# Turning the gathered token rows of a mixture-of-experts kernel by a transposing DMA instead of TensorE

## What is computed

```python
x = x + jnp.tanh(g_xattn[0]) * _L0_xattn_ref(ctx, ctx, _layernorm(x, axis=-1), ssm_kernel, D, 8)
x = x + jnp.tanh(g_ffn[0]) * _L0_ffn_ref(_layernorm(x, axis=-1), gate_w, w1, w2, w3, sw1, sw2, sw3)

# _L0_ffn_ref, 2048 tokens t of 512, 16 experts of 352, top 2, and a shared expert of 704
scores = jax.nn.softmax(t @ gate_w.T, axis=-1)
weights, indices = jax.lax.top_k(scores, TOP_K)
for e in range(N_EXPERTS):
    w_e = jnp.sum(jnp.where(indices == e, weights, 0.0), axis=-1)
    y = y + _swiglu(t, w1[e], w3[e], w2[e]) * w_e[:, None]     # (silu(t @ wa.T) * (t @ wb.T)) @ wo.T
z = _swiglu(t, sw1, sw3, sw2)
return (y + z).reshape(shape)
```

## Time and profile before

| | us |
|---|---|
| median of 3 runs | 742.87 |
| lowest, highest | 742.52, 745.36 |
| span of the profiled execution | 739.8 |
| PE busy | 717.1 (97%) |
| DVE busy | 568.5 (77%) |
| ACT busy | 459.4 (62%) |
| POOL busy | 363.4 (49%) |
| DMA, queue of SP | 89.67 MB, 37.1% of 16 engines |
| DMA, queue of POOL | 24.40 MB, 17.9% of 16 engines |

### The profile page before, as it was taken

One profiled execution on the slowest core, in us unless ns is written; L12 is line 12 of the kernel. 1 busy time (PEld: TensorE's weight loads), 2 busy tenths in 40 slices (PEclk: granted clock), 3 DMA queues, 4 the chain that ended last, 5 costly groups with the idle time before them and its releaser, 6 DMA issues.

```text
span 739.8 us, 15553 instructions
## 1 busy us (share of the span) xinstructions
PE 717.1 (97%) x4602; PEld 676.3 (91%) x4602; DVE 568.5 (77%) x1111; ACT 459.4 (62%) x659; POOL 363.4 (49%) x190
## 2 busy tenths in 40 slices
PE   3999999999999999999999999999999999999998
PEld 3999999999998999899989999988989999999997
DVE  7899999999965578428899588848987699679942
ACT  6575757575432222126878588847885789578931
POOL 4999888887401065042435433543634354434320
PEclk9999999999999999999999999999999999999999
DMA  6678687877522122463667577766565764432101
GB/s 231 215 239 288 218 272 216 279 218 253 186 85 60 29 43 29 144 197 90 161 201 218 131 232 210 198 176 168 145 182 160 176 193 90 74 68 46 30 1 57
DMA packets 48404, 114.88 MB, mean 155 GB/s; under 512 B 7472, under 2 KB 8624, under 8 KB 48336
## 3 DMA queue, kind: packets, MB, share of 16 engines
q1 hardware_dynamic: 35792, 89.67, 37.1%
q0 software_dynamic: 12544, 24.40, 17.9%
HBM read 157.78 MB, written 29.26 MB: 253 GB/s over the span
## 4 chain that ended last, share of the span: by engine, by line
PE 69%; DVE 13%; DMA 6%; issue 5%; ACT 3%; SPq 1%; ACTq 1%; POOL 1%; DVEq 1%; POOLq 0%
PE pair L1303 19%; PE bank L1303 15%; PE pair L1328 12%; PE pair L1234 8%; PE bank L1328 6%; PE bank L1185 4%; PE pair L1311 3%; DMA out<-ys,slot_info 3%; DMA raw<-in_weights 2%; PE bank L1245 2%; DVE prod L829 2%; DVE bank L834 2%; DVE x L800 2%; DVE w_lo L1150 1%; DVE rows L841 1%
## 5 line engine op out<-in xcount | busy, mean ns | idle before, releaser
L1150 DVE TENSOR_TENSOR w_lo<-raw,w_hi 128x1408 fp32r<-128x1408 f32 x94 | 148.5, 1621 | 47.0 <-ACT w_hi L733 47.0
L1441 POOL DMA_INDIRECT out<-ys,slot_info x47 | 80.6, 1714 | 120.6 <-ACT ys L721 87.3
L1428 POOL DMA_INDIRECT tn<-t_rows,slot_info x47 | 75.5, 1605 | 123.1 <-DVE tT_lo L888 90.6
L733 ACT ACTIVATE w_hi<-raw 128x1408 fp32r x94 | 124.6, 1374 | 2.1 <-issue 1.4
L1234 PE MATMUL pair<-kv_hi,toep_hi 128*128 128x288 f32 x320 | 100.6, 314 | 1.7 <-DMA toep_lo<-kpad_lo 1.4
L1234 PE MATMUL pair<-kv_lo,toep_hi 128*128 128x288 f32 x320 | 95.3, 298 | 0.0
L1234 PE MATMUL pair<-kv_hi,toep_lo 128*128 128x288 f32 x320 | 95.1, 297 | 0.0
L1155 DVE TENSOR_TENSOR w_lo<-raw,w_hi 128x1536 fp32r<-128x1536 f32 x47 | 82.3, 1752 | 4.5 <-ACT w_hi L740 4.5
L1379 POOL TENSOR_TENSOR kv_lo<-kv,kv_hi 128x2304 fp32r<-128x2304 f32 x15 | 77.3, 5153 | 5.9 <-ACT kv_hi L625 5.9
L740 ACT ACTIVATE w_hi<-raw 128x1536 fp32r x47 | 69.3, 1474 | 0.1
L829 DVE TENSOR_TENSOR prod<-pair,q 128x256 f32<-128x256 f32 x128 | 53.4, 417 | 15.1 <-PE pair L1234 9.6
(11 more groups left out here) (223 smaller groups left out, 2009.3 us busy)
## 6 DMA issues: line engine op xcount, KB each, us to landing
raw<-in_weights SPq DMA_DIRECT2D x94, 704.0 KB
raw<-in_weights SPq DMA_DIRECT2D x47, 768.0 KB
toep_hi<-kpad_hi SPq DMA_DIRECT2D x15, 512.0 KB, 4.6
toep_lo<-kpad_lo SPq DMA_DIRECT2D x15, 512.0 KB, 6.2
cx<-in_ctx SPq DMA_DIRECT2D x15, 384.0 KB, 6.3
stage<-in_weights SPq DMA_DIRECT2D x16, 272.0 KB, 6.7
xt<-in_x SPq DMA_DIRECT2D x16, 256.0 KB, 6.4
xr<-in_x SPq DMA_DIRECT2D x16, 256.0 KB, 6.6
```

Source lines behind the costliest of these rows:

```text
L733: act.activation(w_hi[s % 2][:, a:b], raw[:, bass.ds(half + a, b - a)], ACT.Copy).then_inc(hi_ok[n_], 1)
L1150: dve.tensor_tensor(w_lo[s % 2][:, a:b], raw[:, bass.ds(half + a, b - a)], w_hi[s % 2][:, a:b].bitcast(F32), ALU.subtract).then_inc(lo_ok[ ...
L1428: pool.indirect_dma_start(out=tn[o % 3][:], out_offset=None, in_=t_rows, in_offset=bass.IndirectOffsetOnAxis(ap=slot_info[:, 3 * i:3 * i + ...
L1441: pool.indirect_dma_start(out=out, out_offset=bass.IndirectOffsetOnAxis(ap=rows, axis=0), in_=ys[o % 2][:], in_offset=None, bounds_check=R ...
```

## The change

The kernel no longer turns the gathered rows on PE. The steps are now:

1. ACT writes each normalized tile a second time as two planes of half words (`halves_of_words`): the low 16 bits of all 512 numbers, then the high ones. The two copies stand between norm_x and q_copy in the turn of the first stage, the last tile's ahead of the second stage's loop. SP stores these planes, and not t1, to t_rows (2048 rows of 1024 half words).
2. POOL gathers rows of planes into fetched (two buffers), in the step of `last_unit(o - 6)`, and waits for the save that frees the buffer.
3. SP saves fetched to one of four DRAM scratch tensors turn_rows (256 rows of 512 half words: each token gives two rows), in the step of `last_unit(o - 5)`, after the gather has landed.
4. SP issues a transposing DMA from turn_rows into tn, in the step of `last_unit(o - 4)`, after the save has landed. The two half words of each number come to lie side by side, so tn then holds the turned tile.
5. ACT and DVE split the tile from tn, as they do for shared tiles. The four products on PE and the bank that they wrote are gone from this path.

Shared tiles are loaded as before.

```diff
-        t_rows = nc.dram_tensor("t_rows", (ROWS, L), F32, kind="Internal").ap()
+        t_rows = nc.dram_tensor("t_rows", (ROWS, 2 * L), U16, kind="Internal").ap()
+        turn_rows = [nc.dram_tensor(f"turn_rows_{n}", (2 * P, L), U16, kind="Internal").ap() for n in range(TURNS)]
...
+        planes = sb2("planes", [P, 2 * L], U16, one)
+        fetched = [sb(f"fetched{n}", [P, 2 * L], U16) for n in range(2)]
...
+        def begun(o, ahead):
+            return max(last_unit(o - ahead), 15)
...
+        def gathers_at(n):
+            return [o for o in range(len(ORDER)) if ORDER[o][0] and begun(o, 6) == n]
+        def saves_at(n):
+            return [o for o in range(len(ORDER)) if ORDER[o][0] and max(begun(o, 5), 16 if ORDER[o][1] < 2 else 17) == n]
+        def turns_at(n):
+            return [o for o in range(len(ORDER)) if ORDER[o][0] and max(begun(o, 4), 16) == n]
...
+                if which == "t":
+                    wait(sp, planes_ok, (t + 1) * 2)
+                    sp.dma_start(t_t[bass.ds(t.v, 1)].rearrange("x p c -> (x p) c"),
+                                 planes[p][:]).then_inc(t_out[p], 16)
+                    return
...
+                for o in saves_at(n):
+                    i = ORDER[o][1]
+                    sp.wait_ge(row_in[i % 2], 16 * (i // 2 + 1))
+                    sp.dma_start(turn_rows[i % TURNS].rearrange("(p h) c -> p (h c)", h=2),
+                                 fetched[i % 2][:]).then_inc(turn_out[i % TURNS], 16)
+                for o in turns_at(n):
+                    i = ORDER[o][1]
+                    sp.wait_ge(turn_out[i % TURNS], 16 * (i // TURNS + 1))
+                    wait(sp, tTl_ok, o - 2)
+                    sp.dma_start_transpose(tn[o % 3][:].bitcast(U16).rearrange("p (c r) -> p c r", c=BLOCKS),
+                                           turn_rows[i % TURNS]).then_inc(tn_in[o % 3], 16)
...
+            def halves_of_words(t):
+                p = t.odd
+                wait(act, t_out[p], t.half() * 16)
+                wait(act, t_ok, t + 1)
+                for h in range(2):
+                    act.activation(planes[p][:, h * L:(h + 1) * L], view(t1[p][:].bitcast(U16), h, [[2, L]]),
+                                   ACT.Copy).then_inc(planes_ok, 1)
...
-                for o in prepares_at(n):
-                    if ORDER[o][0]:
-                        turn_tile(o)
...
-                wait(pool, tTl_ok, o - 2)
-                pool.indirect_dma_start(out=tn[o % 3][:], out_offset=None, in_=t_rows,
+                if i >= 2:
+                    pool.wait_ge(turn_out[(i - 2) % TURNS], 16 * ((i - 2) // TURNS + 1))
+                pool.indirect_dma_start(out=fetched[i % 2][:], out_offset=None, in_=t_rows,
```

More of the change, by code:

```diff
@@ L27 @@
 U32 = mybir.dt.uint32
+U16 = mybir.dt.uint16
 ALU = mybir.AluOpType
@@ L59 @@
 FINALS = 2
+TURNS = 4
 @dataclass(frozen=True)
@@ L290, in program @@
         r_fields, r_info, r_done = sem("r_fields"), sem("r_info"), sem("r_done")
-        tn_in, row_in = [sem(f"tn_in{n}") for n in range(3)], [sem(f"row_in{n}") for n in range(3)]
+        tn_in, row_in = [sem(f"tn_in{n}") for n in range(3)], sem2("row_in")
+        planes_ok, turn_out = sem("planes_ok"), [sem(f"turn_out{n}") for n in range(TURNS)]
         tn_mid_in = sem("tn_mid_in")
-        tile_turned, tTh_ok, tTl_ok = sem("tile_turned"), sem("tTh_ok"), sem("tTl_ok")
+        tTh_ok, tTl_ok = sem("tTh_ok"), sem("tTl_ok")
         up_ok, silu_ok, hid_ok = sem("up_ok"), sem("silu_ok"), sem("hid_ok")
@@ L322, in unit @@
             return UNITS[n] if 0 <= n < N_UNITS else None
+        def begun(o, ahead):
+            return max(last_unit(o - ahead), 15)
         def fills_at(n):
-            def at(o):
-                return max(last_unit(o - 4), 15 if ORDER[o][0] else 0)
-            return [o for o in range(3, len(ORDER)) if at(o) == n]
+            return [o for o in range(3, len(ORDER)) if not ORDER[o][0] and max(last_unit(o - 4), 0) == n]
+        def gathers_at(n):
[4 more added lines that the diff above has]
+            return [o for o in range(len(ORDER)) if ORDER[o][0] and max(begun(o, 4), 16) == n]
         def prepares_at(n):
@@ L354, in tn_count @@
         def tn_count(o):
-            return 16 * sum(ORDER[k][0] == ORDER[o][0] and k not in MID for k in range(o % 3, o + 1, 3))
+            return 16 * sum(k not in MID for k in range(o % 3, o + 1, 3))
         def last_unit(o):
@@ L460, in store @@
                 p = t.odd
-                to, src, ready, done = {"x2": (out_t, x2, x2_ok, x2_out), "t": (t_t, t1, t_ok, t_out),
-                                        "tT": (tT_t, tT, tT_ok, tT_out)}[which]
+                if which == "t":
[3 more added lines that the diff above has]
+                    return
+                to, src, ready, done = {"x2": (out_t, x2, x2_ok, x2_out), "tT": (tT_t, tT, tT_ok, tT_out)}[which]
                 wait(sp, ready, t + 1)
@@ L596, in norm_x2 @@
                 p = t.odd
-                wait(act, t_out[p], t.half() * 16)
+                wait(act, planes_ok, (t - 1) * 2)
                 wait(act, t_turned, t - 1)
@@ L684, in turn @@
                     norm_x(t + 1)
+                if not first:
+                    halves_of_words(t - 1)
+                if not last:
                     q_copy(t + 1)
@@ L694, in tile_hi @@
                 routed, i = ORDER[o]
-                if routed:
-                    act.wait_ge(tile_turned, i + 1)
-                    src = ps_t
-                elif o in MID:
+                if o in MID:
                     act.wait_ge(tn_mid_in, 16 * (MID.index(o) + 1))
@@ L711, in _ @@
             norm_x2(At(TILES - 1))
+            halves_of_words(At(TILES - 1))
             def weigh_out(o):
@@ L1271, in _ @@
             sum_rows(At(TILES - 1), 3)
-            def turn_tile(o):
-                pe.wait_ge(row_in[o % 3], tn_count(o))
-                wait(pe, tTl_ok, o)
-                turn_rows(tn[o % 3], ps_t, tile_turned)
             def parts(hi, lo, whi, wlo):
@@ L1420, in gather @@
             def gather(o):
-                routed, i = ORDER[o]
-                if not routed:
-                    return
+                i = ORDER[o][1]
                 if i == 0:
                     pool.wait_ge(r_done, 1)
-                wait(pool, tTl_ok, o - 2)
-                pool.indirect_dma_start(out=tn[o % 3][:], out_offset=None, in_=t_rows,
+                if i >= 2:
+                    pool.wait_ge(turn_out[(i - 2) % TURNS], 16 * ((i - 2) // TURNS + 1))
+                pool.indirect_dma_start(out=fetched[i % 2][:], out_offset=None, in_=t_rows,
                                         in_offset=bass.IndirectOffsetOnAxis(ap=slot_info[:, 3 * i:3 * i + 1], axis=0),
-                                        bounds_check=ROWS - 1, oob_is_err=False).then_inc(row_in[o % 3], 16)
+                                        bounds_check=ROWS - 1, oob_is_err=False).then_inc(row_in[i % 2], 16)
             def add_out(o):
@@ L1445, in _ @@
             for n in range(N_UNITS + 3):
-                for o in fills_at(n):
+                for o in gathers_at(n):
                     gather(o)
```

2 lines of the change are left out of this document (1 added, 1 removed).

## The result

The changed kernel takes **795.4 us** (median of 4 runs, 790.5 to 799.5) against 743.0 beside it: a ratio of 1.071, with a 95% interval of 1.067 to 1.076. It is slower by 52 us, where the forecast was 755, 12 slower. The time lies in the range and the sign is right, but the loss is four times the forecast's.

What follows compares the result with a forecast made beforehand. The prediction took PE as the bound, with DVE and weight loads close behind. Gain -16, transfers +7 and added waits +21 sum to +12; with span 739.8 and 3.1 to the median, 755 us, range 727 to 808.

Steps and rivals of the forecast that it cites:

- What bounds before: Routed part: PE's queue sets the end at 6.62 us per unit, with DVE at 6.30 close behind.
- The gain, -16: Routed tiles: dropping PE's 47 x 4 turning products saves 16 us, ends 15 and 20.7.
- What is late next is DVE at 6.30: Routed units: without the turns DVE's 6.30 us round limits each unit's gain to 0.32 us, 15.0 in all.
- The half-word copies, nothing: First stage: ACT's two added copies, 1.2 us per tile, hide in its 2.8 us idle for PE; no cost.
- Two transfers, 0.80 + 1.1: DMA engines, per routed tile: save 0.80 us, transposing load 1.1 (0.80 or 1.42); +7 us from 380 to 484.
- the rival with the dear load: The transposing load holds the DMA engines 3 us or more a tile: 800 us, far end 899; chance 0.15.
- The transposing load itself: nothing of its own: Routed tiles: issued two units, 12.6 us, ahead of ACT's split, so its landing adds no wait.
- The added waits, +21: Gather waits for save, scatter queues behind gather, ACT's ys waits for scatter: +21 us, ends 0 and +49.
- per load: Added waits counted for each of 14 weight loads among routed units: 0 to 3.5 us, taken as 1.5.
- In a quiet unit 3.9 us are left: Away from weight loads, the scatter lands with 3.9 us to spare before ACT wants the ys buffer again.
- what would show it: Signs of being right: gathers waiting for saves, scatter waits above 30.4 us, PE gaps behind weight splits, DMA share above 0.85.
- Mostly from 380 to 550: Sign: new PE gaps ahead of up products, behind weight splits, would lie mostly from 380 to 550 us.

Runs made afterwards that it cites:

- the run without turns: The kernel before without PE's four products per routed tile, nothing else added (routed output wrong): 736.3 us, ratio 0.992.
- the third buffer: The changed kernel with three buffers for fetched rows in place of two, all transfers kept: 769.0 us, ratio 1.032.
- both cures: The changed kernel with three buffers for fetched rows and the save ahead of the step's weight loads: 763.2 us, ratio 1.031.
- three ys: The changed kernel with three buffers ys in place of two, nothing else touched: 778.8 us, ratio 1.048.
- the run with plain loads: The changed kernel with three fetched buffers, the save first, and plain loads of the same bytes for the transposing ones (routed part wrong): 753.6 us, ratio 1.011.
- idle transposing loads: The kernel before without PE's turns, plus a transposing load per routed tile into buffers nobody reads: 748.4 us, ratio 1.008.

## Why the prediction was wrong, step by step

**What bounds before: right as far as it went.** PE was the bound. What stood behind it was ranked wrongly.

**The gain, -16: it was 6.0.** The step that failed is "What is late next is DVE at 6.30". Behind 716 us, where the DMA is quieter, the units of the changed kernel do go at 6.21 to 6.22, the full 0.40 faster, for the seven units that the chain shows there. Elsewhere another thing was late before DVE: the chain of scatters, by the trace of the run without turns. That it ate all that is missing is not shown. The prediction had weighed the row of 30.4 us for the added waits, but not for its first term. That row told how little slack was left, and a gain on the chain spends that slack first.

**The half-word copies, nothing: right.** ACT has 16.1 us more work in the first 209 us (144.3 for 128.2), PE's busy time is the same to 0.3 us, and ACT's wait for PE ahead of the copy to q fell from 45.1 to 30.5 us.

**Two transfers, 0.80 + 1.1: it was 0.80 + 1.9.** The save was sized right, by its mean with a plain load. For the transposing load the bounds of 0.80 and 1.42 were too low; only the far end held it, and 1.9 lies at the point, "about 2 us a tile", from which the rival with the dear load was said to decide. By the prediction's own working, 5.0 + 0.80 + 1.9 = 7.7 for a unit of 6.30 gives 14 x 1.4 = 20 us (17 with 4.8 for 5.0) and not 7. Measured alone, the loads cost 12. The time of 795 is near the 800 of that rival, but it did not come about in the rival's way: tn was waited for once only, and plain loads in the same place still took 778. That the time lies in the range is luck in part, since this rival had set the upper end.

**"The transposing load itself: nothing of its own": half right.** Nobody waited for its tile but once, 7.6 us. But its issue holds SP, where weight loads and saves are queued. Its line in the changed kernel (ns, min/median/max):

```profile
L577 SPq DMA_TRANSPOSE tn<-turn_rows x47: 1237/1412/5536, 323.6 to 741.2; - x47
```

The prediction counted SP's waits at the save and at the load, and no time for the issue. A plain save's issue takes 0.36 us by its median. How much of the 12 us is SP's hold and how much the engines' time was not separated.

**The added waits, +21: right in kind, too small, and the step that failed most.** 26 us by the third buffer, 32 by both cures; without the save 37 come back, which is the waits with the save's own traffic. What failed is the count: "per load", 14 steps with 1.5 us, and "In a quiet unit 3.9 us are left". It took a wait near each weight load and free units between. But POOL waited for a save at 23 of 47 gathers, and ACT for a scatter at 20. A save landed in 2.0 to 10.2 us (2.1 to 4.4 was assumed, from the medians of stores of the first stage, where no scatters run) and a scatter in up to 11.9. So the round is often longer than a unit, as at 403.93 above, and then its rate would count and not a delay that the next idle time swallows; the run that was to tell the two apart, with three ys, fell between them. Nor did the terms add, as the cures overlap and landings came later: over the 51 scatters from the first routed tile on the mean time from issue to landing is 5.36 us before, 5.57 without turns and 6.29 in the changed kernel.

**A term that was missing: the clock.** PE's 4414 products are as many in the changed kernel as in the run without turns, but they keep it busy for longer. The first line of either page, the changed kernel first:

```profile
PE 722.4 (91%) x4414; PEld 676.0 (85%) x4414; DVE 568.2 (72%) x1111; ACT 476.3 (60%) x691; POOL 365.8 (46%) x190
```
```profile
PE 701.4 (95%) x4414; PEld 656.5 (89%) x4414; DVE 567.8 (77%) x1111; ACT 458.4 (62%) x659; POOL 371.4 (51%) x190
```

So of the 59.8 us between the two spans (794.5 and 734.7) 21.0 are slower products and 38.8 are idle time. The mean granted clock is 0.963 and 0.998. The windows below show how. The prediction priced a stall at its own length. This isn't a cause beside the others: the stalls bring it, so it is part of what each cure gave back (with both cures PE is busy 708.3 us).

**What stays open.** With both waits cured the changed kernel is at 758 to 763, 22 to 27 us above 736.3. Some 10 of it are the transposing (the run with plain loads). The rest comes with the save, the loads and the gathers; the runs don't divide it among the engines' time, SP's list and scatters that land later.

Of what would show it: gathers waiting for saves, ACT's waits well above 30.4, PE's gaps behind weight splits and a share above 0.85 all came. The share is a weak sign, since idle transposing loads alone bring 0.90. "Mostly from 380 to 550" did not come: 551 to 698 lost 21 us of PE's work too, against 24 in 351 to 551.

## What to carry to other kernels

When work is taken from the bounding engine, look for the chain that runs just behind it, and price the gain against that chain's period, not against the next engine's busy time. When an operation moves to DMA, ask for each of its transfers whose list it stands in, what is queued behind it there, and whether the round that it closes (buffer, landing, next issue) takes longer than one unit; if it does, multiply by all units. A further buffer at the tightest place of such a round is a cheap test; here it gave back more than any other single edit that kept the transfers.

## What the runs showed of the hardware

A transposing load of 256 KB of half words took 1.87 us of sixteen engines' time, in 1056 packets of 248 bytes on average, where a save or a plain load of as many bytes took 0.80 in 144 packets, by the mean of the two. In the changed kernel its issue held SP's queue 1.2 us at least and up to 5.5. Where nobody waited for it, it landed 3.2 to 15.2 us after issue (5.5 by the median). The Trainium skill, Advanced Engine Details and Errata, X-Bar Transpose (TRN2), calls such a load as fast as a regular one: here it took 2.3 times the engine time. The Trainium skill, VectorE: DVE Perf Modes, The three transpose paths, gives 1309 ns for a block by DMA; the eight blocks of a tile are an estimate of 10.5 us by that page. Here that lies among the slow landings and far above the 1.87 us of engine time.

A gap on PE cost more than its length. Here is one in the changed kernel. ACT comes to ys 6.15 us late, for a scatter; its hi parts and DVE's lo parts of the weights are late by that, and PE idles 5.29 us for them. Timeline of ACT and of PE, and windows of 3 us (columns as in the earlier trace rows, the granted clock is the third number from the end):

```profile
585.74 0.69 ACT L765 ACTIVATE ys<-bank,slot_info 128x512 f32<-128x512 f32 x1 [6.15 <-DMA out<-ys,slot_info]
591.38 0.93 PE L1342 MATMUL bank<-w_hi,tT_hi 128*128 128x352 f32 x2 [5.29 <-DVE w_lo L1194]
```

```profile
585.00:588.00 3.00, 1.09 (x5) 0.56 (x3) 0.04 (x1) 2.24 (x3) 1.51 (x1) 1.00 0.53 118
588.00:591.00 3.00, 0.00 (x0) 0.00 (x0) 3.00 (x2) 3.00 (x4) 0.06 (x1) 0.95 0.34 100
591.00:594.00 3.00, 2.62 (x9) 2.65 (x10) 3.00 (x5) 3.00 (x5) 2.16 (x1) 0.50 0.58 167
594.00:597.00 3.00, 3.00 (x12) 3.00 (x11) 3.00 (x3) 2.19 (x2) 1.69 (x1) 0.50 1.07 400
597.00:600.00 3.00, 3.00 (x17) 2.72 (x16) 3.00 (x5) 1.36 (x3) 0.00 (x0) 0.91 0.87 261
```

When PE starts again the granted clock is 0.50, the lower of its two levels (1.2 and not 2.4 GHz), through two windows and into a third. The second of them has 12 products in 3 us, and the one after it, at 0.91, has 17. By an estimate from these rows, half of the some 6 us that PE worked at the lower level, the gap of 5 us cost about 3 more.
